# The last feed-forward with three tile sets, its rounding constants in PSUM, and another order of VectorE's work

## The reference

```python
xb = x.reshape(sh[:-1] + (sh[-1] // BLOCK, BLOCK))
amax = jnp.max(jnp.abs(xb), axis=-1, keepdims=True)
sc = jnp.clip(amax / FP4_MAX * global_scale, 0.0, FP8_MAX)
sc8 = sc.astype(jnp.float8_e4m3fn).astype(jnp.float32)
dq = sc8 / global_scale
a = jnp.clip(jnp.abs(xb) / safe_dq, 0.0, FP4_MAX)
q = jnp.sign(xb) * _FP4_VALS[jnp.digitize(a, _FP4_MIDS)]
...
gate_out = nvfp4_linear(x, gate_w, s_in[0])
up_out = nvfp4_linear(x, up_w, s_in[0])
hidden = jax.nn.silu(gate_out) * up_out
return nvfp4_linear(hidden, down_w, s_in_down[0])
```

## Time and profile before

| | us |
|---|---|
| timed runs, median of 3 | 3663.2 |
| lowest, highest | 3662.15, 3675.84 |
| the profiled execution's own time | 3680.94 |
| its span, first to last instruction | 3679.2 |
| last feed-forward, from its first `L3f_hid` (3428.7) to the end | about 250 |

### The profile page before, as it was taken

The page is one execution under the profiler, slowest core; times in us unless marked ns, Lnnn a source line. Parts: engine busy times, 40 slices in busy tenths (PEclk is TensorE's granted clock), DMA queues, the critical chain, the costliest instruction groups (busy, mean ns, idle before and its releaser), DMA issues. The chain is left out here.

```text
span 3679.2 us, 44806 instructions
## 1 busy us (share of the span) xinstructions
PE 2879.3 (78%) x16749; PEld 1619.2 (44%) x16756; DVE 2067.6 (56%) x3639; ACT 1434.3 (39%) x1900; POOL 1145.0 (31%) x1007
## 2 busy tenths in 40 slices
PE   4888888758867979999866889777999995788333
PEld 2333333533324534444563344366777774233111
DVE  3445455756635735444774666684454442665787
ACT  1254455415552224444413445432333331466211
POOL 2122222221222215555423768740010111122323
PEclk7688899878976979999987899888999997699755
DMA  5454544024521001111100000000211213553000
GB/s 125 73 110 97 117 104 111 19 66 98 115 53 36 1 18 35 41 42 58 58 6 12 1 1 1 24 1 21 96 54 35 72 57 75 93 112 79 20 9 13
DMA packets 129175, 198.50 MB, mean 54 GB/s; under 512 B 35712, under 2 KB 65920, under 8 KB 128832
## 3 DMA queue, kind: packets, MB, share of 16 engines
q1 hardware_dynamic: 97216, 143.23, 17.2%
q0 software_dynamic: 31744, 52.41, 5.2%
HBM read 130.73 MB, written 64.75 MB: 53 GB/s over the span
## 5 line engine op out<-in xcount | busy, mean ns | idle before, releaser
L2127 DVE TENSOR_REDUCE L_mx<-bank_t 128x2 f32<-128x1024 f32 (+3 forms) x512 | 562.8, 1122 | 503.7 <-PE bank_t L1935 309.5
L2333 ACT ACTIVATE L_P<-bank_t 128x1024 f32<-128x1024 f32 (+2 forms) x512 | 478.0, 946 | 485.4 <-PE bank_t L1949 302.3
L2127 DVE TENSOR_REDUCE L2a_mx<-bank_t 128x2 f32<-128x1024 f32 x256 | 311.6, 1223 | 400.8 <-PE bank_t L1912 399.8
L2333 ACT ACTIVATE L2a_P<-bank_t 128x1024 f32<-128x1024 f32 x256 | 261.6, 1023 | 288.5 <-PE bank_t L1924 288.2
L1935 PE MATMUL bank_t<-L_KS,L_QS 48*128 48x512 f32 (+2 forms) x1024 | 264.3, 519 | 102.4 <-DMA L_QS<-L_spill_q_halves 81.9
L1949 PE MATMUL bank_t<-L_QS,L_KS 50*128 50x512 f32 (+2 forms) x1024 | 242.4, 477 | 104.1 <-DVE L_mx L2127 76.7
L1912 PE MATMUL bank_t<-L2a_QK 32*128 32x512 f32 x1536 | 255.2, 447 | 74.0 <-DVE L2a_mx L2127 36.7
L1980 PE MATMUL bank_o<-L_P,L_V 128*32 128x512 f32 (+3 forms) x2048 | 288.6, 640 | 2.6 <-ACT xn L2340 1.8
L1935 PEld LDWEIGHTS bank_t<-L_KS,L_QS 48*128 48x128 f32 x1024 | 109.2, 212 | 353.1 <-issue 245.5
L1920 PE MATMUL bank_t<-L2a_QK 32*128 32x512 f32 x1536 | 257.8, 444 | 0.0
L1912 PEld LDWEIGHTS bank_t<-L2a_QK 32*128 32x128 f32 x1536 | 137.7, 196 | 237.4 <-issue 108.2
(11 more groups left out here) (422 smaller groups left out, 6058.8 us busy)
## 6 DMA issues: line engine op xcount, KB each, us to landing
L_KS<-L_spill_k_halves SPq DMA_DIRECT2D x192, 128.0 KB, 4.5
L_QS<-L_spill_q_halves SPq DMA_DIRECT2D x192, 128.0 KB, 4.9
L_spill_raw<-xn POOLq DMA_DIRECT2D x64, 256.0 KB, 2.5
L2g_raw<-in_L_ffn_h_blocks SPq DMA_DIRECT2D x32, 512.0 KB, 3.9
L_spill_k_halves<-L_hi SPq DMA_DIRECT2D x32, 256.0 KB, 2.0
L_spill_k_halves<-L_lo SPq DMA_DIRECT2D x32, 256.0 KB, 2.3
L_spill_q_halves<-L_hi SPq DMA_DIRECT2D x32, 256.0 KB, 2.5
L_spill_q_halves<-L_lo SPq DMA_DIRECT2D x32, 256.0 KB, 2.9
```

The lines of the kernel that those rows point to most:

```text
L2127: e.tensor_reduce(neg, s.tile[:, :, 0:n_keys], AX.X, ALU.max, negate=True).then_inc(sem(s.done), 1)
L2333: e.activation(s.at.Pr[s.pb][:, :, q0:S], s.tile[:, :, q0:S], ACT.Exp, scale=s.at.scale).then_inc(sem(s.exp), 1)
```

## The change

- `Quantise` is split: `BlockMax` (the maxima) is a step of its own, the nine small operations a second one. `sc8` is now kept negated.
- The rounding constant is made by ScalarE (a Copy with a scale), in this feed-forward's loop into the PSUM pair `bank_t[2]`, one for all items; for the weights and the first `x` item in place in SBUF. The add and the subtract become scalar_tensor_tensor operations that take the maximum with `RNE / 2` on the way; the subtract is turned round, so that `y` is negative as well.
- Three sets of `y`, `mg`, `q` and small tiles in place of two.
- The ring has five banks (0, 1, 2, 3 of `bank_t` 0 and 1, and `bank_o`) in place of seven.
- The list of a round is ordered anew, and the ticks of the attention's end stand singly in four places of rounds 0 to 5, the rest in round 6.

```diff
+                elif kind is BlockMax:
+                    dve.wait_ge(*s.after)
+                    e.tensor_reduce(s.q.small[s.s][:, 0, 0:s.n // BLOCK], s.src.rearrange("p (n k) -> p n k", k=BLOCK), AX.X,
+                                    ALU.max, apply_absolute_value=True).then_inc(sem(s.done), 1)
...
-                    e.tensor_tensor(sc8, sc8, M, ALU.subtract).then_inc(step.sem, 1)
+                    e.tensor_tensor(sc8, M, sc8, ALU.subtract).then_inc(step.sem, 1)
                     dve.wait_ge(step.due())
-                    e.tensor_scalar(inv, sc8, 2.0 ** -10, None, ALU.max).then_inc(step.sem, 1)
+                    e.tensor_scalar(inv, sc8, -1.0, 2.0 ** -10, ALU.mult, ALU.max).then_inc(step.sem, 1)
...
                     e.tensor_scalar(mm.bitcast(I32), yy.bitcast(I32), 0x7F800000, None,
-                                    ALU.bitwise_and).then_inc(step.sem, 1)
+                                    ALU.bitwise_and).then_inc(sem(s.powers), 1)
+                elif kind is RoundFp4:
+                    yy, mm = s.q.y[s.s][:, 0:s.n], s.scaled
+                    dve.wait_ge(*s.after)
+                    e.scalar_tensor_tensor(out=yy, in0=mm, scalar=RNE / 2, in1=yy, op0=ALU.max,
+                                           op1=ALU.add).then_inc(step.sem, 1)
                     dve.wait_ge(step.due())
-                    e.tensor_scalar(mm, mm, 1.0, RNE / 2, ALU.max, ALU.mult).then_inc(sem(s.done), 1)
-                elif kind is RoundFp4:
-                    yy, mm = s.q.y[s.s][:, 0:s.n], s.q.mg[s.s % len(s.q.mg)][:, 0:s.n]
-                    dve.wait_ge(*s.after)
-                    e.tensor_tensor(yy, yy, mm, ALU.add).then_inc(step.sem, 1)
-                    dve.wait_ge(step.due())
-                    e.tensor_tensor(yy, yy, mm, ALU.subtract).then_inc(sem(s.rounded), 1)
+                    e.scalar_tensor_tensor(out=yy, in0=mm, scalar=RNE / 2, in1=yy, op0=ALU.max,
+                                           op1=ALU.subtract).then_inc(sem(s.rounded), 1)
...
+                elif kind is GridSteps:
+                    mm = s.q.mg[s.s % len(s.q.mg)][:, 0:s.n]
+                    act.wait_ge(s.powers, *s.scaled_after)
+                    e.activation(s.scaled, mm, ACT.Copy, scale=RNE / 2).then_inc(sem(s.done), 1)
...
+            item["scaled"] = (q.mg[s % len(q.mg)] if q.bank is None else q.bank)[:, 0:item["n"]]
+            return GridSteps(q, s, item["n"], item["scaled"], [item["read"], q.mg_free[s % len(q.mg)]], due("powers"),
+                             [q.bank_free], item["steps"])
...
             def main(scope, tail):
                 more_tiles(scope, 1)
+                more_tiles(scope, 2)
...
-                f.ring, f.tail = Banks(ALL.aps[:7]), tail
+                f.ring, f.tail = Banks([ALL.aps[i] for i in (0, 1, 2, 3, 6)]), tail
+                q4.bank = bank_t[2].rearrange("p c n -> p (c n)")
...
+                def end_step(k):
+                    if k < 6:
+                        tail.tick()
+                    elif k == 6:
+                        tail.rest()
+
                 hidden_of(0)
                 hidden_of(1)
                 now, turning = scales_of(0), []
+                scales(now[0])
                 for k in range(len(work)):
                     hidden_of(k + 2)
-                    if k == 4:
-                        tail.rest()
-                    elif k < 4:
-                        for _ in range(4):
-                            tail.tick()
+                    end_step(k)
+                    if k >= 2:
+                        turn_it, rounded = turning.pop(0)
+                        turn_it(*rounded)
+                    end_step(k)
+                    item, then = now
                     coming = scales_of(k + 1)
-                    if k >= 2:
-                        then, rounded = turning.pop(0)
-                        then(*rounded)
-                    item, then = now
-                    add(item["scale"])
                     add(grid_steps(item))
+                    if coming is not None:
+                        scales(coming[0])
+                    end_step(k)
                     turning.append((then, round_to_fp4(item)))
+                    end_step(k)
                     now = coming
```

More of the change, by code:

```diff
@@ L130 @@
 WeightMax = namedtuple("WeightMax", "dst src after done")
-Quantise = namedtuple("Quantise", "q src n gs s after inv")
+BlockMax = namedtuple("BlockMax", "q src n s after done")
+Quantise = namedtuple("Quantise", "q n gs s maxed inv")
 ScaleBlocks = namedtuple("ScaleBlocks", "q src n s after done")
-GridSteps = namedtuple("GridSteps", "q s n after done")
-RoundFp4 = namedtuple("RoundFp4", "q s n after q_free rounded done")
+GridSteps = namedtuple("GridSteps", "q s n scaled after powers scaled_after done")
+RoundFp4 = namedtuple("RoundFp4", "q s n scaled after q_free rounded done")
 Turn16 = namedtuple("Turn16", "pieces qo bank after mm dst copy_after done")
@@ L1603, in quantise, with scales @@
         def quantise(q, src, n, gs, after):
-            s = q.count % 2
+            s = q.count % len(q.y)
             q.count += 1
-            e_inv, e_scaled = due("inverse_scales"), due("scaled")
-            add(Quantise(q, src, n, gs, s, [*after, q.y_free[s]], e_inv))
-            return dict(q=q, s=s, n=n, read=e_scaled, scale=ScaleBlocks(q, src, n, s, [e_inv], e_scaled))
+            e_max, e_inv, e_scaled = due("block_maxima"), due("inverse_scales"), due("scaled")
+            add(BlockMax(q, src, n, s, [*after, q.y_free[s]], e_max))
+            return dict(q=q, s=s, n=n, read=e_scaled, scales=Quantise(q, n, gs, s, e_max, e_inv),
+                        scale=ScaleBlocks(q, src, n, s, [e_inv], e_scaled))
+        def scales(item):
+            add(item["scales"])
+            add(item["scale"])
         def grid_steps(item):
@@ L1612, in grid_steps @@
             item["steps"] = due("grid_steps")
-            return GridSteps(q, s, item["n"], [item["read"], q.mg_free[s % len(q.mg)]], item["steps"])
+            item["scaled"] = (q.mg[s % len(q.mg)] if q.bank is None else q.bank)[:, 0:item["n"]]
+            return GridSteps(q, s, item["n"], item["scaled"], [item["read"], q.mg_free[s % len(q.mg)]], due("powers"),
+                             [q.bank_free], item["steps"])
         def round_to_fp4(item):
             q, s, n = item["q"], item["s"], item["n"]
-            st = RoundFp4(q, s, n, [item["steps"]], q.q_free[s], due("fp4_rounded"), due("fp4_ready"))
+            st = RoundFp4(q, s, n, item["scaled"], [item["steps"]], q.q_free[s], due("fp4_rounded"), due("fp4_ready"))
             add(st)
-            q.mg_free[s % len(q.mg)] = st.rounded
+            q.mg_free[s % len(q.mg)] = q.bank_free = st.rounded
             q.y_free[s] = st.done
@@ L1636, in quantiser @@
             q.y, q.mg, q.qq, q.small, q.count = y, mg, qq, small, 0
-            q.q_free, q.y_free, q.mg_free = [None, None], [None, None], [None] * len(mg)
+            q.bank, q.bank_free = None, None
+            q.q_free, q.y_free, q.mg_free = [None] * len(qq), [None] * len(y), [None] * len(mg)
             return q
@@ L1708, in quantised_weights @@
                 item = quantise(q, raw[r], S, col[:, 3 * w + 1:3 * w + 2], [e_raw, fp4_ready[n]])
-                add(item["scale"])
+                scales(item)
                 raw_free[r] = item["read"]
@@ L1789, in begin @@
                     state["item"], state["turn"] = x_part(0)
-                return [lambda: x_norm(0), begin, lambda: add(state["item"]["scale"]),
+                return [lambda: x_norm(0), begin, lambda: scales(state["item"]),
                         lambda: add(grid_steps(state["item"])), lambda: state.update(out=round_to_fp4(state["item"])),
```

15 lines of the change are left out of this document (7 added, 8 removed).

## The result

| timed runs, us | before | changed | ratio (95% interval) |
|---|---|---|---|
| first pairs | 3675.8 (3660.9 to 3692.4, 7 runs) | 3633.8 (3624.0 to 3648.5, 7 runs) | 0.989 (0.9863 to 0.9916) |
| a second time | 3675.8 (3665.9 to 3693.2, 11 runs) | 3646.6 (3631.8 to 3668.4, 6 runs) | 0.9909 (0.9878 to 0.9939) |

The account below looks back on a forecast made before the run. VectorE, busy 81% of the last feed-forward, was taken as the bound. The terms summed to -29.9 us from the median 3663.2, giving 3633.3; the 8-in-10 range was 3615 to 3649.

Parts of the forecast that it names:

- 1 constant's operation: Last feed-forward: making the rounding constant leaves VectorE for ScalarE, 19 operations of 0.73 us, -13.9.
- 2 waits for GpSimd: Last feed-forward: maxima stop waiting (-14.3), L2241 no longer stretched (-8.0), three clamps lose 0.45 each (+1.4): -20.9.
- 4 order: VectorE's list: two starts per tile no longer follow an operation whose result they read, 0.1 us each: -3.6.
- 6 end: Last item: clamp waits less for GpSimd's L3f_y, -2.1; ScalarE's constant is uncovered there, +1.05.
- Term 5: Attention's end: VectorE's 7.02 us projection wait goes, other waits come: -2.3 (-7 to +2); reciprocal's operand later, +0.4.
- Term 7: Five banks: down projection waits for a bank, delaying the addition to X in nine rounds: +9.5 (+5.0 to +12.7).
- term 3: VectorE's add and subtract with a maximum take 1.27 us against 1.23, 38 times: +1.7 (0 to +7.6).
- 8 elsewhere: Stage's start -0.4; layer before, weight pieces +0.5 and one piece without +0.2.
- second rival: TensorE stays at 1.2 GHz, so projections and bank waits are all slow: -24.3 in all, 3639 us; chance 0.13.
- first rival: The down projection's wait before the addition to X doesn't show: -40, 3623 us; chance 0.20.
- third rival: GpSimd's L3f_y and VectorE's new add and subtract exclude each other: +35 on the forecast, 3668 us; chance 0.07.
- fourth rival: Layer before: ScalarE's copy delays L2g_w_high by 5.45 us in 12 pieces, in full +65, 3698 us; chance 0.04.

Follow-up runs that it names:

- experiment 7: The changed kernel with the attention's end in its old places (four steps at the head of rounds 0 to 3, rest in round 4): stage 224.69 us against 220.94.
- experiments 6: The changed kernel with the constants in SBUF and seven banks in the ring: stage 236.44 us, against 249.40 with constants in SBUF and five banks.
- 8: The changed kernel with the addition to X behind the block maxima on VectorE: stage 207.90 us against 220.94.
- 9: The changed kernel with bank_m as a sixth bank in the ring from round 7: stage 210.90 us against 220.94.
- experiment 5: The changed kernel with the constants in SBUF in place of PSUM, still five banks: stage 249.40 us against 220.94.
- experiment 1: The kernel before with three sets of tiles in place of two, nothing else: stage 249.73 us against 250.46.

## Why the prediction was right

The forecast for the stage was about -30, measured -29.5. Terms 1, 2, 4 and 6 hold one by one. Terms 5 and 7 came out dearer, and term 3 and a gain in no term made up for that.

| term | forecast | in the trace after |
|---|---|---|
| 1 constant's operation | -13.9 | -13.9, the group is gone |
| 2 waits for GpSimd | -20.9 | -14.3 and 19 x (0.672 - 0.248) = -8.1; three clamps of 1.18 or 1.19 for 0.68, +1.5 |
| 3 add and subtract | +1.7 | 19 x (1.218 + 1.224 - 2 x 1.226) = -0.2 |
| 4 order | -3.6 | clamp 1.13 behind the maxima's start, where L2241 came at 1.25; likewise the first small operation: 18 x 2 x 0.12 = -4.3 |
| 5 attention's end | -2.3 + 0.4 | 0.67 + 5.06 + 0.11 + 0.81 for 7.02 + 0.88: -1.3; and +0.9, below |
| 6 end | -2.1 + 1.05 | clamp +1.62 for a wait of 3.71, ScalarE 1.09: -1.0 |
| 7 five banks | +9.5 | 9 x 1.32 = +11.9 |
| 8 elsewhere | +0.3 | +0.7, the wait of 0.66 at the stage's start; in the layer before nothing is seen |
| not in the sum | | -1.1, the first small operation of three normalisations, below |

The right column sums to -29.2; 0.3 of the 29.5 is not assigned. That the total came so close is partly luck: terms 5 and 7 were 1.5 and 2.4 too good, terms 3 and 4 were 2.6 too bad, and the 1.1 was in no term.

*Term 3* was drawn as a line through two short forms, and that line doesn't hold at 1024 columns: the operation costs there what the tensor_tensor of the earlier trace rows did.

*Term 5* was mis-sized in three places. The first is a wait of before that it left out, the one ahead of the next addition to `X`:

```profile
3485.19 0.48 DVE L2283 SCALAR_TENSOR_TENSOR X<-bank_o,L3f_cols,X 128x256 f32<-128x256 f32 x1 [0.88 <-PE bank_o L1874]
```

The second is the clock: the second projection took 3.73, not 1.99. In the trace after TensorE waited 4.59 ahead of the first projection and 2.23 between the two, and ran both at the slow form; the matmuls behind, from 3463.96, are fast. In experiment 7, with 0.78 between them, the second took 1.99, as before. What raises the clock in time I can't tell from these rows. So the hidden tile waited 5.06 and not 3.2. The third is that `L_OT` (3452.73, 1.59 us) now lies beside the powers operation, which took 1.63 instead of 0.69 (+0.9). It is the same exclusion that the prediction had read from L2241, at a place where it hadn't looked.

*In no term* was the same exclusion at the normalisation. Its first small operation on VectorE (L2064, 128x4) took 0.17, 0.43 and 1.02 us in the stage of before; the one of 1.02 starts at 3555.07 beside an `L3f_y` that ends at 3556.07. In the changed kernel all three take 0.17.

*Term 7* took the middle between the two clocks. All nine projections with a wait ran at 1.89, though the mean granted clock of the stage was the same 0.62: the mean doesn't tell at which level a given projection runs. The wait was 1.32 (1.41 by my chain). The second rival had this part right, all rounds slow; its total for the difference, -24.3, was not reached: terms 3 and 4 fell on the good side by 2.6, and the rest lies in the 0.88 and 1.1 above and in the two matmul groups of the attention's end, which ran at the fast clock. The first rival (no wait shows) is out: experiments 6, 8 and 9 give the wait back as 13.0, 11.3 and 9.3 us.

*The third rival*, exclusion between `L3f_y` and the two new operations, is out for the changed kernel and real without its PSUM operand: experiment 5 costs 28.5 where the rival had 35, since a tile loses 1.5 on VectorE and not the whole 1.93.

*The fourth rival*, ScalarE held in the layer before, didn't come about. ScalarE's timeline there:

```profile
2666.89 0.63 ACT L2405 ACTIVATE XT<-XT 128x512 f32<-128x512 f32 x1 [1.56 <-DVE XT L2286]
2667.43 1.04 ACT L2391 ACTIVATE L2g_w_high<-L2g_raw 128x1024 fp32r<-128x1024 f32 x1
```

ScalarE waits for the powers and `L2g_w_high` comes later, but from the first to the last of these the layer takes 542.2 us (543.5 in the second profile), and 542.1 and 542.0 in the two of before. The other kernels show 542.0 to 548.3, with and without the copy on ScalarE (546.8 in experiment 1, which has none).

The experiments also show what the sum of terms doesn't: the parts aren't independent. The third set alone brings 0.7, and with it left out of the new order 6.6 are lost. The constant on ScalarE alone costs 10.0, and back on VectorE in the new order, with its output in PSUM, 22.2. It takes the new order, in which GpSimd's `L3f_y` goes ahead of `L3f_q` and the nine small operations stand between powers and add, to make both of use. And the order brought its own cost, the addition to `X` right behind the hidden tile, which one move gives back. No run has the new order by itself, with two sets and the constant on VectorE, so what it is worth alone stays open.
